# Output projection of a chunked attention scan: weight held, 512 columns moving, turned back once a segment

## The reference, cut to what matters

```python
def step(carry, inp):
    mem, z = carry
    q_s, k_s, v_s, qn_s, kn_s = inp
    scores = jnp.einsum('bhnd,bhmd->bhnm', q_s, k_s) * SCALE
    scores = jnp.where(mask, scores, -jnp.inf)
    sdpa = jnp.einsum('bhnm,bhmd->bhnd', jax.nn.softmax(scores, axis=-1), v_s)
    sq = elu1(qn_s)
    num = jnp.einsum('bhnk,bhkv->bhnv', sq, mem)
    den = jnp.einsum('bhnk,bhk->bhn', sq, z)[..., None]
    out = beta * num / (den + 1e-06) + (1.0 - beta) * sdpa
    sk = elu1(kn_s)
    prev_v = jnp.einsum('bhnk,bhkv->bhnv', sk, mem) / jnp.einsum('bhnk,bhk->bhn', sk, z)[..., None]
    mem = mem + jnp.einsum('bhnk,bhnv->bhkv', sk, v_s - prev_v)
    z = z + sk.sum(axis=2)
    return (mem, z), out
_, outs = jax.lax.scan(step, (mem0, z0), (qs, ks, vs, qnope, knope))
out = outs.transpose(1, 0, 3, 2, 4).reshape(B, N, INNER) @ w_out     # [.., 1024] @ [1024, 128]
```

## Time and profile before

| | us |
|---|---|
| median of 3 runs (lowest, highest) | 3374.51 (3370.74, 3388.3) |
| the profiled execution's own time | 3378.05 |
| its span, first to last instruction | 3376.2 |
| of it the scan, to the end | about 1436 |

### The profile page before, as it was taken

One profiled execution on the slowest core, in us unless ns is written; L12 is line 12 of the kernel. 1 busy time (PEld: TensorE's weight loads), 2 busy tenths in 40 slices (PEclk: granted clock), 3 DMA queues, 4 the chain that ended last, 5 costly groups with the idle time before them and its releaser, 6 DMA issues. The chain is left out here.

```text
span 3376.2 us, 133974 instructions
## 1 busy us (share of the span) xinstructions
PE 2890.8 (86%) x56049; PEld 1694.1 (50%) x56049; DVE 2501.5 (74%) x7471; ACT 1930.5 (57%) x3909; POOL 1697.3 (50%) x1600
## 2 busy tenths in 40 slices
PE   5675999999999999997233299999999999999998
PEld 2332333333333333336222167676677767676776
DVE  4567788887888888866660678788888788787876
ACT  4564778787787878772000155555555555555553
POOL 4663000000000000003016499999999999898996
PEclk9777899999999999998565599999999999999999
DMA  3467333333233333309201200000000000000000
GB/s 123 169 207 231 70 83 85 89 77 87 75 85 84 87 87 76 87 25 286 82 27 29 74 4 11 11 11 11 11 11 11 11 11 11 10 7 9 11 7 11
DMA packets 179424, 210.31 MB, mean 62 GB/s; under 512 B 28608, under 2 KB 140288, under 8 KB 178560
## 3 DMA queue, kind: packets, MB, share of 16 engines
q1 hardware_dynamic: 176256, 200.31, 21.3%
q0 software_dynamic: 2560, 1.35, 0.4%
HBM read 125.17 MB, written 75.63 MB: 59 GB/s over the span
## 5 line engine op out<-in xcount | busy, mean ns | idle before, releaser
L778 ACT ACTIVATE at_pA<-at_ps 128x512 f32<-128x512 f32 x1024 | 569.1, 608 | 131.6 <-DVE at_ps L831 131.1
L840 DVE CUSTOM_DVE_ANT_0 at_junk<-at_ps,w_cmask 128x512 f32<-128x512 f32 (+3 forms) x1024 | 462.7, 488 | 169.9 <-PE at_ps L682 169.9
L658 POOL CAST at_mrow<-at_neg 16x128 bf16<-16x128 f32 x64 | 18.0, 282 | 1110.3 <-DVE at_neg L803 1110.3
L831 DVE TENSOR_TENSOR at_ps<-at_ps,w_ratio 128x128 f32<-128x128 f32 (+3 forms) x1024 | 490.4, 493 | 67.2 <-PE at_ps L676 67.0
L784 ACT ACTIVATE at_pB<-at_ps 128x512 f32<-128x512 f32 (+1 forms) x768 | 395.9, 538 | 77.3 <-PE at_ps L692 76.8
L2099 ACT ACTIVATE sc_ee<-sc_ps 128x512 f32<-128x512 f32 x256 | 153.0, 598 | 497.9 <-PE sc_ps L1955 496.5
L676 PE MATMUL at_ps<-at_aq,at_ak 72*128 72x512 bf16 x1024 | 355.9, 391 | 3.5 <-DMA at_ak<-parts_scratch 3.1
L1919 POOL TENSOR_TENSOR sc_rb<-sc_rb,v_sin 128x512 f32<-128x512 f32 x256 | 327.0, 1278 | 48.5 <-DVE sc_ra L2143 48.1
L682 PE MATMUL at_ps<-at_bk,at_bq 72*128 72x512 bf16 (+3 forms) x1024 | 273.2, 309 | 52.3 <-DMA at_bk<-parts_scratch 31.6
L1955 PE MATMUL sc_ps<-sc_xT,v_wqkv 128*128 128x512 f32 x512 | 293.1, 655 | 18.8 <-DVE sc_ra L2143 16.6
L689 PE MATMUL at_ps<-at_bq,at_bk 75*128 75x512 bf16 (+3 forms) x1024 | 283.3, 303 | 18.3 <-DVE at_mx L840 17.3
(11 more groups left out here) (315 smaller groups left out, 6377.9 us busy)
## 6 DMA issues: line engine op xcount, KB each, us to landing
parts_scratch<-fr_parts SPq DMA_DIRECT2D x64, 384.0 KB, 4.1
at_bq<-parts_scratch SPq DMA_DIRECT2D x192, 96.0 KB
at_bk<-parts_scratch SPq DMA_DIRECT2D x192, 96.0 KB
at_aq<-parts_scratch SPq DMA_DIRECT2D x192, 96.0 KB
at_ak<-parts_scratch SPq DMA_DIRECT2D x192, 96.0 KB
v_scratch<-fr_v SPq DMA_DIRECT2D x32, 352.0 KB, 4.3
at_v<-v_scratch SPq DMA_DIRECT2D x32, 352.0 KB, 3.5
parts_scratch<-fr_parts SPq DMA_DIRECT2D x32, 256.0 KB, 3.9
```

Of the source, the lines that this page charges most:

```text
L778: act.activation(pA[:, n % A_RING, j * S:(j + 1) * S], src, ACT.Exp).then_inc(exped, 1)
L831: dve.tensor_tensor(src[:, 0:wide], src[:, 0:wide], W["ratio"][:, S - wide:S], ALU.mult).then_inc(tilted, 1)
L840: ins = dve.tensor_tensor_reduce(junk[:, P * j * (j + 1) // 2:P * (j + 1) * (j + 2) // 2], src[:, col:col + wide], W["cmask"][:, S - wide: ...
```

## The change

`project_out` swaps its operands: `w_out` of the pair is the stationary side and all 512 columns of `oT` move in one matmul, into the same bank 7, which now holds the transposed product (output feature x row). It is called once a step, where the first half stood; the second call is gone. When the eighth pair of a segment is in, ScalarE copies bank 7 into the new SBUF tile `yT` (semaphore `yt_c`), at the end of its step. TensorE turns `yT` back with four transposes (`turn_y`, semaphore `yt`) at the end of the next step, into one of the rotating banks 0 and 1, of which it becomes a further user. VectorE adds that bank to `y`, one step later than before. The loop has one step more (PT + 5).

```diff
--- before.py
+++ after.py
@@ -1713,12 +1713,12 @@
         mx, sm = sb("mx", [P, GH]), sb("sm", [P, 4, GH])
         rk, rq = sb("rk", [P, GH]), sb("rq", [P, GH])
         t1, t2 = sb("t1", [P, 2, GH, DH]), sb("t2", [P, 2, GH, DH])
-        oT = sb("oT", [P, 2, S])
+        oT, yT = sb("oT", [P, 2, S]), sb("yT", [P, S])
         ps = ctx.enter_context(nc.psum_tensor("sc_ps", [P, 8, 512], F32))
 
 
         names = ("h_in0 h_in1 stat fact shift_d xn_d tq_d xnn_d xq_d step xt xt_c xqt xqt_c hb_d ffn ffn_c vp v_c pj ex mn rp sn sg add_d sS skt skc "
-                 "sx se pt pvd old kr_s qr_s kd ud qd od up mu ott otc oproj ydone stored0 stored1").split()
+                 "sx se pt pvd old kr_s qr_s kd ud qd od up mu ott otc oproj yt_c yt ydone stored0 stored1").split()
         G = {n: sem(n) for n in names}
         h_seg = c["h_d"].rearrange("(g f) (s i) d -> f s i g d", f=B1, i=SEG)
         o_seg = out.rearrange("(g f) (s i) d -> f s i g d", f=B1, i=SEG)
@@ -1851,7 +1851,7 @@
                     take_xq(act, 1, 0, 1)
 
         PT = PER * PAIRS
-        STEPS = PT + 4
+        STEPS = PT + 5
         inside = lambda p: 0 <= p < PT
         starts = range(0, PT, PAIRS)
 
@@ -1878,6 +1878,8 @@
                     user(("x", j), "xt_c", j)
                 for j in at_step(s, 6):
                     user(("xq", j), "xqt_c", j)
+                if s - 12 in starts:
+                    user(("y", (s - 12) // PAIRS), "ydone", (s - 12) // PAIRS + 1)
                 if s - 7 in starts:
                     user(("ffn", (s - 7) // PAIRS), "ffn_c", (s - 7) // PAIRS + 1)
             bank_of = lambda *key: users[key] % 2
@@ -2025,13 +2027,17 @@
                             ins = pe.transpose(ps[:, 6, g * P:(g + 1) * P], ol[:, p % 4, g].rearrange("p h d -> p (h d)"), V["ident"][:])
                         ins.then_inc(G["ott"], 1)
 
-                    def project_out(p, gs):
+                    def project_out(p):
+                        wait(pe, "otc", p + 1)
+                        wait(pe, "yt_c", p // PAIRS)
                         h = p % PAIRS
-                        for g in gs:
-                            ins = pe.matmul(ps[:, 7, g * P:(g + 1) * P], oT[:, p % 2, g * P:(g + 1) * P], V["wout"][:, h],
-                                            start=(h == 0 and g == 0), stop=(h == PAIRS - 1 and g == BG - 1))
-                        if BG - 1 in gs:
-                            ins.then_inc(G["oproj"], 1)
+                        pe.matmul(ps[:, 7, :], V["wout"][:, h], oT[:, p % 2], start=(h == 0), stop=(h == PAIRS - 1)).then_inc(G["oproj"], 1)
+
+                    def turn_y(bank, j):
+                        wait(pe, "yt_c", j + 1)
+                        for g in range(BG):
+                            ins = pe.transpose(ps[:, bank, g * P:(g + 1) * P], yT[:, g * P:(g + 1) * P], V["ident"][:])
+                        ins.then_inc(G["yt"], 1)
 
                     for s in range(STEPS):
                         if s < PT:
@@ -2050,10 +2056,7 @@
                         if inside(p):
                             local(p)
                         if inside(s - 4):
-                            wait(pe, "otc", s - 3)
-                            if (s - 4) % PAIRS == 0:
-                                wait(pe, "ydone", (s - 4) // PAIRS)
-                            project_out(s - 4, (0, 1))
+                            project_out(s - 4)
                         if inside(s - 1):
                             score(s - 1)
                         if s < PT:
@@ -2070,8 +2073,6 @@
                             wait(pe, "sx", min(s, PT))
                             wait(pe, "mu", 2 * p)
                             update(p, (0, 1))
-                        if inside(s - 4):
-                            project_out(s - 4, (2, 3))
                         if inside(p):
                             turn_heads(p, s)
                             wait(pe, "mu", 2 * p + 1)
@@ -2082,6 +2083,10 @@
                         for j in at_step(s, 6):
                             free_bank(pe, "xq", j)
                             turn_xq(pe, bank_of("xq", j), j)
+                        if s - 12 in starts:
+                            j = (s - 12) // PAIRS
+                            free_bank(pe, "y", j)
+                            turn_y(bank_of("y", j), j)
                         if s - 7 in starts:
                             j = (s - 7) // PAIRS
                             free_bank(pe, "ffn", j)
@@ -2129,6 +2134,11 @@
                             take_x(act, bank_of("x", j), j, j)
                         for j in at_step(s, 6):
                             take_xq(act, bank_of("xq", j), j, j)
+                        p = s - 4
+                        if inside(p) and p % PAIRS == PAIRS - 1:
+                            wait(act, "oproj", p + 1)
+                            wait(act, "yt", p // PAIRS)
+                            act.copy(yT[:], ps[:, 7, :]).then_inc(G["yt_c"], 1)
 
                 @block.vector
                 def _(dve):
@@ -2212,12 +2222,11 @@
                             wait(dve, f"stored{j % 2}", 64 * (j // 2))
                             dve.scalar_tensor_tensor(flat(y[:, j % 2]), ps[:, bank_of("ffn", j), :], V["qs"][:, 4:5], flat(hb[:, j % 2]),
                                                      ALU.mult, ALU.add).then_inc(G["ffn_c"], 1)
-                        p = s - 4
-                        if inside(p) and p % PAIRS == PAIRS - 1:
-                            j = p // PAIRS
-                            wait(dve, "oproj", p + 1)
+                        if s - 12 in starts:
+                            j = (s - 12) // PAIRS
+                            wait(dve, "yt", j + 1)
                             wait(dve, "ffn_c", j + 1)
-                            dve.tensor_tensor(flat(y[:, j % 2]), flat(y[:, j % 2]), ps[:, 7, :], ALU.add).then_inc(G["ydone"], 1)
+                            dve.tensor_tensor(flat(y[:, j % 2]), flat(y[:, j % 2]), ps[:, bank_of("y", j), :], ALU.add).then_inc(G["ydone"], 1)
 
         clear(nc, sems)
         prepare(0)
```

## The result

The changed kernel takes 3396.74 us (median of 18 runs, 3387.48 to 3401.08) against 3375.67 for the kernel before (18 runs beside them). The ratio is 1.0058, 95% interval 1.0047 to 1.0068: slower by 0.6%, where 1.3% was forecast. The profiled execution took 3397.55 us, span 3395.8, 19.6 more than the span before.

The account below looks back on a forecast made before the run. The prediction took a queue of TensorE bursts to bound the scan, with one wait for ScalarE's key copy hidden behind it. Terms 40 + 8 + 1 + 1 - 6 = +44 us on the 3374.5 median gave 3418 us, range 3388 to 3437.

Parts of the forecast that it names:

- the sign given 83%: Whole kernel: slower by more than the 0.5% (17 us) a measurement can tell from no change, chance 83%.
- (g): TensorE's instruction supply: fewer records and a longer burst before the score shrink issue holes, 6 us gained, bounds 0 and 16.
- (a): TensorE's output projection: one burst of 1.06 us replaces 0.64 and 0.55, saving 0.13 a step, 17 us over 128 steps.
- (b): Projection's place: +0.42 us a step before the score, wait for key copy exposed, 0.06 won back; net +0.36.
- the bound at which nothing is won back: Upper bound on the projection's place: +0.42 us a step, 54 us if all 128 steps count.
- (c): Odd projection, one step in eight: TensorE's wait for VectorE swallows the added 0.42, so 112 steps count: 40 us.
- (d): Turning back at the end of a step: 16 times four transposes cost 8 us, plus 1 us for bank waits behind.
- (f): Kernel's end: copy, transposes and two handoffs now stand between the last projection and VectorE's addition, +1.3 us.
- R2: Rival, instruction supply: holes shrink much more, 16 us for the score and 10 for the rest; 3398 us, chance 14%.
- The step on held weights: TensorE's projection: holding the weight saves hardly more than a second burst's start; six further weight loads cost 0.03 to 0.04 us.
- R4: Rival, TensorE's weight loads: they are the hidden price, three quarters would go, 100 us; 3318 us, chance 3%.
- R1: Rival, TensorE's busy time alone decides, the key copy wait is absorbed elsewhere: 3367 us, not slower, chance 8%.

Follow-up runs that it names:

- before_project_twice: Kernel before with the odd projection's matmul issued twice in every step; 3447.18 us, ratio 1.0220 to the kernel before.
- four_first: Kernel before with both halves of its output projection in front of the score, no held weight, no turning back; 3397.86 us, ratio 1.0055 to before.
- held_by_128: Changed kernel with its 512-column projection matmul split into four of 128 columns with the same weight; 3404.19 us, ratio 1.0068 to the kernel before.
- held_second: Changed kernel with its projection burst moved between the first memory update and the turning of the heads; 3392.27 us, ratio 1.0040 to before.
- four_second: Kernel before with both projection halves between the first memory update and the turning of the heads; 3395.85 us, ratio 1.0049 to before.
- both kernels with the early copy: ScalarE's copy of the turned keys moved ahead of the exponential: on the changed kernel 3377.37 us (1.0015 to before), on the kernel before 3375.41 (1.0000).

## Why the prediction was wrong

It had the direction and the place as its cause: 3418 was forecast, 3396.7 came, inside the range and with the sign given 83%. The size of the change is off by a factor of two (+44 forecast, +21 measured), and what failed is the supply of instructions, term (g).

- (a), (b): +46 forecast, +46.7 measured (table above). 1.06 us for the burst, 2.73 from L1973 to L2027, a clean step of 10.90: each as stated. That the sums agree to a us is partly luck: these bursts held some 6 us of gaps that closed, and without them they make +53, near the bound at which nothing is won back. More was won back in delayed steps than 0.06: the mean distance from L1973 to L2027 fell from 2.92 to 2.75 us, 21 us over the scan. before_project_twice, where the second half still stands in its old place, has the same 21 us, so closed gaps alone can give them; how much of it in the changed kernel is a hole hidden under the wait, no run separates.
- (c): VectorE's wait in the eighth step swallowed 3 us (15.5 to 12.7) instead of 6.
- (d), (f): turning back 0.49 x 15 = 7.4 and nothing visible behind it, for 8 + 1. At the end, from the projection's start to VectorE's addition, 2.6 us against 1.2: +1.4 for 1.3. The changed kernel's last rows:

```profile
3388.91 1.13 PE L2034 MATMUL sc_ps<-sc_oT,v_wout 128*128 128x512 f32 x2
...
3390.08 0.59 ACT L2141 COPY sc_yT<-sc_ps 128x512 f32<-128x512 f32 x1 [1.39 <-PE sc_ps L2034]
...
3390.80 0.63 PE L2039 MATMUL sc_ps<-v_ident,sc_yT 128*128 128x128 f32 x4 [0.77 <-ACT sc_yT L2141]
3391.47 0.69 DVE L2229 TENSOR_TENSOR sc_y<-sc_y,sc_ps 128x512 f32<-128x512 f32 x1 [1.72 <-PE sc_ps L2039]
```

- (g), instruction supply: 6 us forecast with a bound of 16, **35 measured** (62.9 to 28.0). This is the failed step. I had seen that the holes lie whole blocks of 256 records apart, but then costed only the 37 in the score and the share of records. What I should have asked is how long a block lasts: 2.8 blocks a step at 10.5 us leave 3.8 us each, little above the 3.2 to 3.4 of the closest fetches; and the blocks aren't alike, 150 of 340 are used up in under 3.5. At that point almost any time a step gains comes partly out of gaps. On the path it came to 36 us (15.0 in the score, 21.4 between recall and L2027), where 6 in (g) and 7 won back in (b) were forecast: that is 23 us more than forecast, against the 21 between 3418 and 3397. R2 named exactly this and gave 3398, with 16 us for the score where 15 came; I gave it 14%. Its counterargument, that records per us stay almost the same, doesn't hold: they fell from 67.9 (712 over 10.48) to 64.2 in a clean step (700 over 10.90), 5%, and 3% over the whole scan.

The Trainium skill (Runtime: NRT & Kernel Launch, Instruction fetch mechanics) says that instructions are refilled in blocks of 256 and that the cost of crossing a block's boundary is mostly hidden. The blocks of 256 agree with the trace. "Hidden" doesn't for this scan: gaps of over 0.1 us stand at 102 of the 150 boundaries behind blocks used up in under 3.5 us, and at 41 of the other 190.

The step on held weights held: eight weight loads against two made 0.03 us a burst (four_first and held_by_128 at 1.09, the changed kernel at 1.06), so R4 is out. R1 is out by the wait, which L2027 shows in full.

## What to carry to other kernels

Where a TensorE stream of small matmuls nearly uses up its instruction supply, as in this scan, the cost of moving a burst is not its length. Divide the step by its blocks of 256 records, semaphore instructions counted, and see which long, record-poor bursts stand between dense ones. Don't take such a burst out from between dense ones (held_second and four_second did, and their gaps nearly doubled), and save records in the dense stretches. A wait that TensorE shows there was worth less than its length in both kernels with the early copy, and idle time that a change adds is partly paid by gaps that close.

## What of the hardware was unexpected

- TensorE's instruction blocks (16384 bytes, 256 records with the semaphore instructions) come at least 3.22 us apart in all 16 traces, and a gap ends some 2.6 us after the latest fetch began, in the traces with many gaps. Why a fetch that takes 1.07 us has such a spacing stays open.
- A float32 burst over 512 columns costs nearly the same with the weight held (1.05 to 1.06 us) and with four stationary tiles (1.09).
- A burst on the full array is about 0.1 us longer when quarter-array matmuls follow than when full ones do: 0.64 against 0.55 for four instructions, 1.06 against 0.96 for two of 512 columns (held_second, in front of the transposes). The other way round it is the same: local attention on quarters takes 1.03 us in front of the projection and 0.93 in front of the quarter masks (held_second).
